# Forming the x-block differences on GpSimd instead of VectorE in a convolution and gated low-rank FFN kernel

## The reference, cut to what matters

```python
out = lax.conv_general_dilated(x, weight, (1,), [(4, 4)], feature_group_count=4) + ctx + bias
q = out @ Wq_w.T;  scores = q @ keys.T
top_vals, top_idx = top_k(scores, 16)
gate = one_hot(top_idx) weighted by softmax(top_vals)
z = (out @ A_w.T).reshape(..., 64, 8)
y = x + ((z * gate[..., None]).reshape(..., 512) @ B_w.T) * 2.0
```

## Time and profile before

| what | value |
|---|---|
| three timed runs | 233.68, 234.31, 234.09 us; median 234.09 us |
| span of the profiled execution | 232.1 us; no device time of that execution itself is given, so the median stands 2.0 us above its span |
| TensorE busy, granted clock | 227.8 us (98% of the span), 1.000 |
| VectorE busy | 194.5 us (84%) |
| ScalarE busy | 99.5 us (43%) |
| GpSimd busy | 1.5 us (1%), 10 instructions |
| DMA | 38.79 MB, 167 GB/s over the span |

### The profile page before, as it was taken

One profiled execution on the slowest core, in us unless ns is written; L12 is line 12 of the kernel. 1 busy time (PEld: TensorE's weight loads), 2 busy tenths in 40 slices (PEclk: granted clock), 3 DMA queues, 4 the chain that ended last, 5 costly groups with the idle time before them and its releaser, 6 DMA issues.

```text
span 232.1 us, 4019 instructions
## 1 busy us (share of the span) xinstructions
PE 227.8 (98%) x1381; PEld 203.3 (88%) x1381; DVE 194.5 (84%) x471; ACT 99.5 (43%) x246; POOL 1.5 (1%) x10
## 2 busy tenths in 40 slices
PE   7999999999999999999999999999999999999995
PEld 7898998898989889898998989889898989898884
DVE  2799899999999899998999899898998979847232
ACT  4997768246262352525334262532536242101000
POOL 2000000000000000000000000000000000000000
PEclk9999999999999999999999999999999999999999
DMA  6999064742744628173462825538281343554532
GB/s 199 372 406 395 25 194 127 274 133 93 211 151 104 218 82 270 60 211 144 95 235 74 252 82 148 187 88 263 67 272 69 60 169 90 186 145 130 180 135 92
DMA packets 23781, 38.79 MB, mean 167 GB/s; under 512 B 2768, under 2 KB 11856, under 8 KB 23760
## 3 DMA queue, kind: packets, MB, share of 16 engines
q1 hardware_dynamic: 23616, 38.45, 51.5%
q10 hardware_dynamic: 144, 0.08, 0.2%
HBM read 25.94 MB, written 12.58 MB: 166 GB/s over the span
## 4 chain that ended last, share of the span: by engine, by line
PE 90%; ACT 6%; DMA 2%; issue 1%; SPq 0%; DVE 0%; ACTq 0%
PE p_z L646 35%; PE p_out L684 13%; PE p_out L685 13%; PE p_out L692 13%; PE p_conv L600 10%; ACT h_c L395 3%; PE p_out L646 3%; PE p_conv L543 3%; DMA x_blk<-in_x_blocks 2%; ACT x_hi L359 1%; ACT a_hi L359 1%; PE p_z L668 1%; ACT h_hi L359 0%; PE p_z L692 0%; PE p_z L684 0%
## 5 line engine op out<-in xcount | busy, mean ns | idle before, releaser
L684 PE MATMUL p_out<-b_hi,zt_hi 128*128 128x512 f32 (+1 forms) x128 | 50.1, 392 | 0.0
L685 PE MATMUL p_out<-b_hi,zt_lo 128*128 128x512 f32 (+1 forms) x128 | 50.1, 392 | 0.0
L692 PE MATMUL p_out<-b_lo,zt_hi 128*128 128x512 f32 (+1 forms) x128 | 34.4, 391 | 0.0
L646 PE MATMUL p_z<-a_hi,h_lo 128*128 128x264 f32 x240 | 34.2, 285 | 0.0
L646 PE MATMUL p_z<-a_hi,h_hi 128*128 128x264 f32 x240 | 34.1, 285 | 0.0
L646 PE MATMUL p_z<-a_lo,h_hi 128*128 128x264 f32 x240 | 33.9, 284 | 0.0
L646 PEld LDWEIGHTS p_z<-a_hi,h_hi 128*128 128x128 f32 x240 | 32.0, 188 | 1.6 <-issue 0.4
L646 PEld LDWEIGHTS p_z<-a_hi,h_lo 128*128 128x128 f32 x240 | 31.3, 188 | 0.0
L646 PEld LDWEIGHTS p_z<-a_lo,h_hi 128*128 128x128 f32 x240 | 31.0, 188 | 0.0
L685 PEld LDWEIGHTS p_out<-b_hi,zt_lo 128*128 128x128 f32 x128 | 24.0, 188 | 5.6
L684 PEld LDWEIGHTS p_out<-b_hi,zt_hi 128*128 128x128 f32 x128 | 24.0, 188 | 5.6
(11 more groups left out here) (105 smaller groups left out, 258.1 us busy)
## 6 DMA issues: line engine op xcount, KB each, us to landing
x_nat<-in_x_rows SPq DMA_DIRECT2D x16, 512.0 KB, 5.0
out_dram<-x_nat SPq DMA_DIRECT2D x31, 256.0 KB, 3.3
x_blk<-in_x_blocks SPq DMA_DIRECT2D x14, 516.0 KB, 4.0
z_dram<-a_raw SPq DMA_DIRECT2D x64, 64.0 KB, 1.8
a_raw<-z_dram SPq DMA_DIRECT2D x16, 256.0 KB, 3.7
a_raw<-in_a_wq SPq DMA_DIRECT2D x8, 264.0 KB, 6.1
x_nat<-in_b_w SPq DMA_DIRECT2D x4, 512.0 KB, 8.6
x_blk<-in_x_blocks SPq DMA_DIRECT2D x2, 258.0 KB, 3.6
```

Source lines behind the costliest of these rows:

```text
L646: mm = nc.tensor.matmul(z_bank(t, b)[:, 0:HB], h[:, t % 2, r, :], a[:, r, b * HB:(b + 1) * HB], start=k == 0 and r == 0, stop=k == 2 and r ...
L684: nc.tensor.matmul(dst, zt_hi[:, t % 2, c, :], b_hi[:, c, cols], start=c == 0, stop=False)
L685: nc.tensor.matmul(dst, zt_lo[:, t % 2, c, :], b_hi[:, c, cols], start=False, stop=False)
L692: mm = nc.tensor.matmul(dst, zt_hi[:, t % 2, c, :], b_lo[:, c, start:stop], start=False, stop=c == JC - 1)
```

## The change

The two differences of each tile from 5 to 15, 22 instructions in all, leave VectorE's program and stand in GpSimd's, in the order of tiles, behind the last of its set-up instructions. GpSimd waits for the landing of the tile (`x_come(t)`) and then forms both. Operands, results, the semaphore `s_xd` and its values are the same. No other instruction is added, and SyncE's program is the same.

```diff
@@ block.gpsimd
+            def differ(t, ab):
+                if ab == 0:
+                    pool.wait_ge(*x_come(t))
+                blocks = x_blk[:, t % XB]
+                nc.gpsimd.tensor_tensor(blocks[:, XS + ab * XO:XS + (ab + 1) * XO], blocks[:, ab * NN:ab * NN + XO],
+                                        blocks[:, XE:XS], ALU.subtract).then_inc(s_xd, 1)
+
+            for t in range(TW, NT):
+                differ(t, 0)
+                differ(t, 1)
@@ block.vector
-            def differ(t, ab):
-                if ab == 0:
-                    dve.wait_ge(*x_come(t))
-                blocks = x_blk[:, t % XB]
-                nc.vector.tensor_tensor(blocks[:, XS + ab * XO:XS + (ab + 1) * XO], blocks[:, ab * NN:ab * NN + XO],
-                                        blocks[:, XE:XS], ALU.subtract).then_inc(s_xd, 1)
...
             sum_w(1)
-            differ(5, 0)
-            differ(5, 1)
             split_ws(1)
...
             for i in range(3, NT):
-                if i + 3 < NT:
-                    differ(i + 3, 0)
                 copy_scores(i)
                 top_first(i)
-                if i + 3 < NT:
-                    differ(i + 3, 1)
                 take_first(i)
```

## The result

The changed kernel is slower: 243.25 us median of four runs (240.57 to 245.01) against 234.03 of the kernel before; the ratio is 1.034, 95% interval 1.027 to 1.041. The ratio leaves out the run of 245.01, which was disturbed; times 234.03 it makes 242.0 us, 8.0 more. The profiled execution took 243.3 us with a span of 241.5, so 9.4 more than the span of before.

The account below looks back on a forecast made before the run. TensorE, busy 227.8 of 232.1 us, was taken to bound the kernel. Removal 0, start +1.4 and middle +1.5 gave +2.9: span 235.0, plus 2.0 from span to median, 237.0 us; range over all 233.8 to 243.0.

Parts of the forecast that it names:

- TensorE bounds the kernel, and the removal is worth nothing: Whole kernel: TensorE waits for no difference, so taking 22 instructions, 14.8 us, off VectorE gains 0.
- A GpSimd difference takes 1.29 us: On GpSimd: each two-input 128 x 512 instruction takes 1.29 us, with 0.69 us as the lower end.
- The engines exclude each other in reading: SBUF: a VectorE instruction with two SBUF inputs and a GpSimd one block each other, at the full price; without it 0.
- The start, +1.4 us: Tiles 5 and 6: GpSimd delays e_top twice, 1.56 us; z_g of tile 2 comes late, TensorE waits 1.4 us once.
- The middle, 5 x 0.3 = +1.5 us: Middle iterations: in five of nine, GpSimd's first difference delays h_lo, then q_t; TensorE waits 0.3 us each, 1.5 us.
- Rival (a): Middle iterations: a waiting GpSimd goes ahead of q_t; with the start +12.6 us, 246.7; chance 0.21, whole or in part.
- The range: Total time over all cases: 233.8 to 243.0 us; the forecast's own range is 234.4 to 239.
- x_hi, SyncE's queue and the clock: Elsewhere: x_hi has 6.1 us for 2.6 us of work, SyncE's queue keeps its order, TensorE runs at full granted clock.

Follow-up runs that it names:

- the run without the differences: Kernel before, but VectorE forms only the differences of tiles 5 to 7 and nobody those of 8 to 15: 234.22 us against 234.17, ratio 0.9998.
- one-input copy of 1030 columns: Kernel before, all differences on VectorE, plus two unneeded one-input GpSimd copies for each tile from 5 to 15: 241.41 us, ratio 1.0308.
- the memset that costs nothing: Kernel before, all differences on VectorE, plus two unneeded GpSimd memsets of 1320 columns for each tile from 5 to 15: 234.29 us, ratio 1.0007.
- the run with the start alone: Against the kernel before, GpSimd forms the differences of tiles 5 and 6 only, VectorE all others in their old places: 235.85 us, ratio 1.0078.

## Why the prediction was right in sign and short in size

The forecast was 237.0 us, 2.9 more than before. The ratio of the runs gives 242.0, 8.0 more, and the profiled execution 9.4 more. Blocking and its direction were foreseen; most of its size was not.

- *TensorE bounds the kernel, and the removal is worth nothing.* Right, by the run without the differences: 0.9998.
- *A GpSimd difference takes 1.29 us if each input costs a column's time.* Right: 1.29 us where nothing stood in its way. With the second input for free it would have been 0.69. The working behind it, 1.16 ns for each column read, doesn't hold in general: a one-input copy of 1030 columns took 1.05 us where it gives 1.29.
- *The engines exclude each other in reading, where VectorE reads two SBUF operands.* Right, by q_t, h_lo and zt_lo in the trace, and by the memset that costs nothing.
- *The start, +1.4 us.* 1.6 us in the trace, 1.8 by the run with the start alone. The size was right, its bearer wrong, and that the sum agrees is partly luck. I had e_top caught twice; in this execution tile 5 landed about 1 us later than before, and GpSimd began on tile 6 at 37.05 in place of the 35.8 that I had reckoned. e_top was missed, and h_lo (1.71 in place of 1.18 us) and zt_lo (1.76 in place of 0.65) were caught; TensorE lost most of it waiting for zt_lo, where I had z_g. In the run with the start alone e_top was caught once, and others after it, for about the same loss. VectorE has two-input work all along there, so in these two executions it hardly mattered which is met.
- *The middle, 5 x 0.3 = +1.5 us.* Here the prediction failed. It took q_t to follow h_lo without letting a waiting GpSimd in, because q_t starts 0.09 us before h_lo has ended. The trace shows the two engines taking turns: q_t stood behind a whole difference (1.35 to 1.38 us) in eight of the nine iterations, and the middle cost 7.5 us (0.6 + 6.9) in place of 1.5. The 0.3 us itself was reckoned from the weight load at 105.59; the product itself begins at 105.82, 0.2 later, so the wait of a load is not all lost: three loads that waited 0.57 us cost 0.3 to 0.4. Rival (a) had this mechanism, with 11.2 us for the middle; it was too high by 3.7. One of the nine iterations missed h_lo and q_t (GpSimd began at 80.37, when q_t was ending), which is 0.8, and q_t ends 0.14 us after its turn comes and not 0.35, its start being behind it, which is 1.7 in eight iterations; the remaining 1.2 us are not taken apart.
- *The range.* It reached to 243.0; the median of the runs is 243.25, the ratio makes it 242.0. Rival (a) deserved more than 0.21: I gave the order of turns away on an overlap of 0.09 us that says nothing of who is let in next.
- *x_hi, SyncE's queue and the clock.* As forecast, none of them plays a part: TensorE never waits for x_hi, and the granted clock is unchanged.

## What to carry to other kernels

Before work goes from VectorE to GpSimd, list VectorE's instructions with two SBUF inputs that lie around the moment at which the GpSimd work will be released, and ask which of them somebody waits for. Each pair of neighbours there can cost up to a whole GpSimd instruction, since the engines take turns (1.2 to 1.5 us an iteration here where both differences came in between). "As soon as the data has landed" is the wrong moment if there are microseconds to spare: releasing it by the last critical instruction left no loss that can be told (0.2%) here, in place of 2.9%. And if the engine that sets the time waits for nothing of VectorE's, the move has nothing to win.

## What the runs showed of the hardware that I had not expected

- The engine that waits gets the next turn, even against an instruction that follows on the other engine without a gap: q_t, begun 0.08 us before h_lo had ended, stood still for a whole GpSimd difference. In the profile a standing instruction shows as a long one (q_t 1.38 in place of 0.35 us) and not as a wait, so VectorE's busy time rose by 2.6 us while 14.8 us were taken from it.
- How long VectorE stands still follows the length of the GpSimd instruction: q_t took 1.38 us behind a difference of 1.29 and 1.13 behind a copy of 1.05. The copy reads 1030 columns and the difference 2 x 512, so at 1.05 against 1.29 us the columns read do not alone set the time.
- 8.8 us less on VectorE gave nothing in the kernel before, but with GpSimd reading at the same moments, keeping the differences on VectorE, where they stood still as well (1.05 in place of 0.68 us), went with a loss of 12.4 us in place of 8.0.
